# Four fused transformer blocks on one core: the first feed-forward's quantisation chain, its output bias, and the start of the second attention, reordered

## The chip, the cores and the metric

The kernel runs on one core of one Trainium2 chip. The metric is the device time of the program in microseconds (us); the kernel before takes 862.85 us (median of 3 runs, 858.54 to 864.74). One more execution was profiled; all traces here are of that one.

## The reference

Sixteen images of 16x16 tokens with 96 channels (4096 tokens) go through four blocks. Each block adds a mixing layer and a feed-forward to the residual, both on a layer norm of it. The mixing layers are: attention in windows of 16 tokens (3 heads of 32), attention in 8x8 windows, and two Fourier mixers, the second with weights routed per image; the feed-forwards of blocks 2 to 4 are mixtures of 4 experts (2 used). The change concerns mostly block 1's feed-forward, two "bit linear" layers with quantised activations:

```python
def _quantize_activations_groupwise(x):      # 5 groups of rows; the 16th image stays zero
    for g in range(5):
        gamma = max(|x[g]|)                  # one number for a whole group of 3 images
        x[g] = clip(x[g] * 128 / (gamma + 1e-5), -128 + 1e-5, 128 - 1e-5)
h   = quantise(x @ sign(W1 - mean).T + b1)   # 96 -> 384
out = quantise(gelu(h) @ sign(W2 - mean).T + b2)   # 384 -> 96
```

Each group's maximum must be known over all of its tokens before any of its values can be used, twice. In block 4 the mixer's weights come from a small network on each image's mean: `routing = softmax((scale * relu(mean @ fc1)**2 + bias) @ fc2)`.

## The kernel before

The residual X stays in SBUF for the whole program (128 tokens by 96 channels in each of 32 tiles). Five instruction streams are written out by hand, one for each of TensorE (PE), VectorE (DVE), ScalarE (ACT), GpSimd (POOL) and the DMA queue of SyncE (SP). Each runs strictly in its written order, and semaphores alone order the streams against each other. So the order in which a stream is written decides what waits behind what.

Attention, mixers and expert layers run over 8 groups of 4 tiles (512 tokens), as a software pipeline: in the pass for group g, TensorE works on g-1, g and g+1, and statistics and layer norms are made for g+2 and g+3. A layer norm (`normalise`, L472 to L496) is a chain of eleven POOL instructions that waits for DVE's statistics (`bn_stats`, L895 for 4 tiles, L912 for 6); TensorE then transposes its result (L1401 for 4 tiles, L1424 for 6).

The first feed-forward runs over 5 groups q = 0 to 4 of 6 tiles (FG, FT), in a loop written in each stream. For group q:
- `ffn_stats(q)` on DVE, `normalise` on POOL, `ffn_turn(q)` on PE, `ffn_hi` on ACT (L608) and `ffn_lo` on DVE (L917) split the normalised input in two parts.
- `ffn_up(q, j)`, j = 0 to 5 (L1434, L1435): first product; `ffn_y1` on ACT (L675) moves it out of PSUM and adds b1.
- First scale: `first_max` on DVE three times (L924), a small reduce (L1119), a PE transpose of the 128 row maxima (L1623), the maximum of that row on DVE (L1123), a PE product with ones that spreads it to all partitions (L1626), three small DVE instructions (L1132 to L1136), then three clips (L1140).
- gelu on ACT, three times (L697), then `down(q, t)`, t = 0 to 5: the bias b2 by a product with ones (L1565) and the second product (L1568). `ffn_out` on ACT (L681) copies it to the one buffer Y2.
- Second scale: the same chain again, one step later in the loop: L1084, L1578, L1088, L1582, L1092 to L1095, clip L1097, and L1099 adds the result to X.

In pass q of the loop DVE does `ffn_lo(q + 1)` first, the first scale of group q, and, in between, the second scale of group q - 2. TensorE does `ffn_up(q + 1)`, `down(q - 1)` and the products of both chains. After the loop come the last second scales, and then `attention(2, 1)`: it begins on DVE with the statistics of its group 2 and the softmax of group 0 (maximum L947, subtraction L953, exponential on ACT L625, sum L959, division L965).

Mixer 3 (block 4, `mixer3` in each stream) has, per group, a routing chain: `route_in` on PE (L1838), `routing_relu` on ACT (L815, L817), `routing_star` on DVE (L1293), `route_logits` on PE (L1847). On ACT `routing_relu` stands behind `mix_image(g, p, 0)` (L780), which waits for the first half of `mix_dft` on PE (L1754); on DVE `routing_star` is the last of the pass, behind `mix_x` (L1256) and `routing_out` (L1317); on PE `route_logits` is the last of the pass, right behind `mix_dft`.

Of the kernel before, what the change touches and what calls it, by code (L numbers as in the profile page):

```python
# [24 lines left out]
GT = 4  # L25
# [26 lines left out]
def program(nc, a, out):  # L52
    ctx = ExitStack()
    with ctx:
# [68 lines left out]
        gmx = sb("gmx", [1, 2])  # L123
# [4 lines left out]
        Y2 = sb("Y2", [P, FT, C])  # L128
# [70 lines left out]

        FT_BANKS = (slice(0, 2), slice(5, 7))  # L200

        def turned(m):
# [11 lines left out]
        CW = Y2[0:NF].rearrange("p t c -> p (t c)")[:, 0:8 * HF]  # L214
# [30 lines left out]
        ft_pe, fh_a, fl_v, fu_pe, y1_a, ab_v, gm1_v, gm2_v, g1_pe, g2_pe = (  # L245
            sem(n) for n in ("ft_pe", "fh_a", "fl_v", "fu_pe", "y1_a", "ab_v", "gm1_v", "gm2_v", "g1_pe", "g2_pe"))
        qs1_v, qs2_v, zero_p, y2_a = (sem(n) for n in ("qs1_v", "qs2_v", "zero_p", "y2_a"))
# [52 lines left out]
        def after(eng, s, value):  # L300

            if not (isinstance(value, int) and value <= 0):
                eng.wait_ge(s, value)

# [47 lines left out]
        def _(sp):  # L352
            with nc.allow_non_contiguous_dma(reason="small weights"):
# [11 lines left out]
                sp.wait_ge(zero_p, 1)  # L365
                sp.dma_start(b2bc[0:1, :], a["L0_ffn_b2"].rearrange("(a n) -> a n", a=1)).then_inc(wffn, 16)
# [100 lines left out]
        def _(pool):  # L467
            pool.memset(b2bc[:], 0.0).then_inc(zero_p, 1)
# [115 lines left out]
        def _(act):  # L584
# [93 lines left out]
            def ffn_out(q):  # L678
                act.wait_ge(fd_pe, 2 * q + 2)
                after(act, xu[1], q)  # L680
                act.activation(Y2[:].rearrange("p (u t) c -> p u (t c)", u=2), PS[:, 3:5, 0:3 * C], ACT.Copy).then_inc(y2_a, 1)  # L681
# [3 lines left out]
            for q in range(FG):  # L685
# [14 lines left out]
            act.activation(qT[0:C, :], bank(0, 512, C), ACT.Copy, scale=QSCALE).then_inc(q_a, 1)  # L700
# [141 lines left out]
            def mixer3(g, p):  # L842
# [24 lines left out]
        def _(dve):  # L867
# [58 lines left out]
            def attention(phase, ka, prev):  # L926
# [12 lines left out]
                def body(g, p):  # L939
                    n, m = 8 * ka + g, 8 * ka + g  # L940
                    if has(g, 3, 2, PREPS[phase]):
# [3 lines left out]
                    if has(g, 1):  # L945
# [11 lines left out]
                    if has(g, 1):  # L957
# [15 lines left out]
                    if ka == 0 and isinstance(g, int):  # L973
# [108 lines left out]
            def second_max(r):  # L1082
                dve.wait_ge(y2_a, r + 1)
                dve.tensor_reduce(am1[:, 1:2], Y2[:], AX.XY, ALU.max, apply_absolute_value=True).then_inc(gm2_v, 1)  # L1084

            def second_row(r):
                dve.wait_ge(g2_pe, 2 * r + 1)
                dve.tensor_reduce(gmx[:, 1:2], PS[0:1, 7, 256:256 + P], AX.X, ALU.max).then_inc(gm2_v, 1)  # L1088

            def second_scale(r):  # L1090
                dve.wait_ge(g2_pe, 2 * r + 2)
                dve.tensor_scalar(qe[:, 1:2], PS[:, 7, 384:385], QEPS, 1.0 / QB, ALU.add, ALU.mult).then_inc(qs2_v, 1)  # L1092
                dve.wait_ge(qs2_v, 2 * r + 1)
                dve.reciprocal(qs[:, 1:2], qe[:, 1:2])
                dve.tensor_scalar(ql[:, 1, :], qc[:], qe[:, 1:2], None, ALU.mult).then_inc(qs2_v, 1)  # L1095
                dve.wait_ge(qs2_v, 2 * r + 2)
# [901 lines left out]
```

## Time and profile before

| | us |
|---|---|
| median of 3 runs | 862.85 |
| profiled execution | 860.89 |
| its span, first to last instruction | 859.1 |
| busy in the span: PE, DVE, POOL, ACT | 779.6, 589.5, 556.4, 428.5 |
| first feed-forward, first clip to the first transpose of attention 2 that follows it | 98.03 to 167.37 |
| mixer 3, first to last `route_logits` of its loop | 631.4 to 693.7 |

The rows further down come from views of one trace. A timeline row gives the start and the length of a run of like instructions, and in brackets how long the engine stood idle before it and what released it. A row of groups gives count, busy time, mean nanoseconds, and the idle time before. A row of stretches gives, for each engine, busy time and count, and the TensorE clock granted (PEclk: 1.00 is 2.4 GHz, 0.50 is 1.2 GHz).

### The profile page before, as it was taken

How to read it: one execution, taken by the hardware profiler on the slowest of the kernel's cores; microseconds unless marked ns; L12 is line 12 of the kernel's file. 1: busy time of each engine (PE TensorE's matmuls, PEld its weight loads, DVE VectorE, ACT ScalarE, POOL GpSimd, SP SyncE). 2: the span in 40 equal slices, each digit the busy share in tenths (PEclk: the TensorE clock that was granted, in tenths of full speed). 3: DMA queues.
4: the chain of work that ended last, by engine and by line, in shares of the span. 5: the costliest groups of instructions: out<-in, count | busy, mean ns of one | idle time of the engine just before them, and what ended most of it. 6: DMA issues, size and time to landing. Idle time of an engine off the chain costs nothing.

```text
span 859.1 us, 27761 instructions
## 1 busy us (share of the span) xinstructions
PE 779.6 (91%) x10760; PEld 641.8 (75%) x10760; DVE 589.5 (69%) x1609; ACT 428.5 (50%) x777; POOL 556.4 (65%) x885
## 2 busy tenths in 40 slices
PE   4897678699899999969997999999799999999996
PEld 3776566588688888958876688888777776888886
DVE  6677477678577777848874477787776773776754
ACT  3564563366544444457773553535445555444441
POOL 5645523455287887867773687788565674788764
PEclk9696698799999999989998999999967999999999
DMA  6611100000311101000011011010000011110030
GB/s 165 125 12 30 35 1 2 2 3 3 78 54 36 50 28 29 3 1 2 0 46 30 28 31 30 27 56 3 2 1 2 0 29 29 33 55 27 28 84 20
DMA packets 39145, 26.17 MB, mean 30 GB/s; under 512 B 27132, under 2 KB 31981, under 8 KB 39045
## 3 DMA queue, kind: packets, MB, share of 16 engines
q1 hardware_dynamic: 38302, 24.41, 11.2%
q8 instruction: 68, 1.11, 0.6%
q10 hardware_dynamic: 742, 0.38, 0.2%
q14 instruction: 33, 0.26, 0.1%
HBM read 7.87 MB, written 1.57 MB: 11 GB/s over the span
## 4 chain that ended last, share of the span: by engine, by line
PE 81%; DVE 10%; ACT 3%; issue 3%; POOL 2%; POOLq 0%; ACTq 0%; DVEq 0%
PE PS L1679 22%; PE PS L1652 9%; PE PS L1653 8%; PE PS L1656 4%; PE PS L1401 3%; PE PS L1767 3%; PE PS L1754 3%; PE PS L1387 3%; PE PS L1778 2%; PE PS L1787 2%; PE PS L1388 2%; PE PS L1797 2%; PE PS L1568 2%; PE PS L1480 2%; PE PS L1847 1%
## 5 line engine op out<-in xcount | busy, mean ns | idle before, releaser
L712 ACT ACTIVATE H<-PS,B 128x512 f32<-128x512 f32 x288 | 173.7, 690 | 194.7 <-PE PS L1656 194.7
L1679 PEld LDWEIGHTS PS<-M,H 128*64 128x64 f32 x4608 | 192.3, 137 | 21.7 <-issue 17.5
L1679 PE MATMUL PS<-M,H 128*64 128x96 f32 x4608 | 205.1, 248 | 1.8 <-DVE X L1196 1.8
L1196 DVE SCALAR_TENSOR_TENSOR X<-PS,G,X 128x96 f32<-128x96 f32 (+1 forms) x384 | 121.7, 318 | 96.6 <-PE PS L1679 86.3
L480 POOL TENSOR_TENSOR msum<-stats 128x4 f32<-128x4 f32 (+1 forms) x61 | 16.1, 263 | 137.7 <-DVE stats L895 111.3
L1652 PE MATMUL PS<-XH,M1h 128*128 128x512 f32 x192 | 78.7, 410 | 0.0
L490 POOL TENSOR_TENSOR XN<-X,mean 128x384 f32<-128x384 f32 x56 | 47.0, 840 | 48.9 <-PE PS L1401 48.9
L1653 PE MATMUL PS<-FHL,M1l 128*128 128x512 f32 x192 | 77.3, 402 | 0.0
L516 POOL TENSOR_TENSOR PF<-G,B 128x1536 f32<-128x1536 f32 x24 | 66.2, 2759 | 10.2 <-DVE G L1187 10.2
L524 POOL TENSOR_TENSOR ex<-euler,dl 128x16 f32<-128x16 f32 x24 | 69.9, 2912 | 1.7 <-DVE dl L1160 1.6
L494 POOL TENSOR_TENSOR rs<-ve,half 128x4 f32<-128x4 f32 (+1 forms) x61 | 65.4, 1072 | 4.8
L1401 PE MATMUL PS<-ident,XN 128*96 128x128 f32 x224 | 39.8, 307 | 17.3 <-POOL XN L496 17.3
L895 DVE BATCH_NORM_STATS2 stats<-X 128x6 f32<-128x96 f32 (+1 forms) x224 | 41.1, 244 | 15.0 <-POOL XN L496 12.6
L496 POOL TENSOR_TENSOR XN<-XN,rs 128x384 f32<-128x384 f32 x56 | 47.4, 847 | 4.4
L604 ACT ACTIVATE XH<-PS 96x512 fp32r<-96x512 f32 x56 | 33.1, 591 | 33.4 <-PE PS L1401 33.0
L900 DVE TENSOR_TENSOR XL<-PS,XH 96x512 fp32r<-96x512 f32 x56 | 38.1, 680 | 16.7 <-ACT XH L604 16.7
L551 POOL TENSOR_TENSOR H<-H 96x128 f32<-96x128 f32 x64 | 29.6, 492 | 28.3 <-DVE H L1345 28.3
L1652 PEld LDWEIGHTS PS<-XH,M1h 128*128 128x128 f32 x192 | 36.7, 191 | 13.4 <-ACT H L712 5.4
L1652 PE MATMUL PS<-FHL,M1h 128*128 128x512 f32 x96 | 43.5, 453 | 3.2 <-ACT H L712 3.2
L530 POOL TENSOR_TENSOR X<-X,PF 128x384 f32<-128x384 f32 (+1 forms) x24 | 24.3, 1012 | 32.5 <-DVE X L1196 32.5
L519 POOL TENSOR_TENSOR PF<-PF 128x768 f32<-128x768 f32 x24 | 43.7, 1823 | 1.9
L1156 DVE TENSOR_TENSOR gs<-gs 128x16 f32<-128x16 f32 x24 | 42.8, 1782 | 0.8
(245 smaller groups left out, 1818.3 us busy)
## 6 DMA issues: line engine op xcount, KB each, us to landing
FHL<-XH SPq DMA_DIRECT2D x36, 192.0 KB, 2.5
FHL<-XL SPq DMA_DIRECT2D x36, 64.0 KB, 2.1
X<-XH SPq DMA_DIRECT2D x12, 192.0 KB, 2.5
raw<-L_ffn_w SPq DMA_DIRECT2D x3, 576.0 KB, 5.1
M<-L_ffn_w SPq DMA_DIRECT2D x3, 576.0 KB, 5.0
XH<-XL SPq DMA_DIRECT2D x24, 64.0 KB, 1.9
out<-X SPq DMA_DIRECT2D x8, 192.0 KB, 2.6
X<-x SPq DMA_DIRECT2D x3, 384.0 KB, 6.7
```

The source lines that it names most:

```text
L490: pool.tensor_tensor(xn, x, rows(mean), ALU.subtract).then_inc(part, 1)
L494: pool.tensor_tensor(rs[:, 0:n], ve[:, 0:n], half[:, 0:n], ALU.pow).then_inc(part, 1)
L496: pool.tensor_tensor(xn, xn, rows(rs), ALU.mult).then_inc(done, 1)
L516: pool.tensor_tensor(GB, G[:].unsqueeze(3).to_broadcast([P, GT, EXP, C]), B2[e][:].unsqueeze(1).to_broadcast([P, GT, EXP, C]), ALU.mult).t ...
L519: pool.tensor_tensor(GB[:, :, 0:2, :], GB[:, :, 0:2, :], GB[:, :, 2:4, :], ALU.add).then_inc(gb_p, 1)
L524: pool.tensor_tensor(ex[:, :, :].rearrange("p t e -> p (t e)"), euler[:], dl[:, :, :].rearrange("p t e -> p (t e)"), ALU.pow).then_inc(gex ...
L712: act.activation(H[p][:, c, :], bank(UB[c]), ACT.Gelu, bias=B1[e][:, c:c + 1]).then_inc(gelu_a, 1)
L1196: ins = dve.scalar_tensor_tensor(xt(g, t), bank(4 + t % 2)[:, e * C:(e + 1) * C], G[:, t, e:e + 1], xt(g, t), ALU.mult, ALU.add)
L1401: ins = pe.transpose(o, XN[:, t, :], ident[:])
L1652: pe.matmul(bank(UB[c]), M1h[e][:, cs], XS[p][j], start=True, stop=False)
L1653: pe.matmul(bank(UB[c]), M1l[e][:, cs], XS[p][k], start=False, stop=False)
L1679: ins = pe.matmul(Y[rows, x * C:(x + 1) * C], H[p][:, j, t * P + rows.start:t * P + rows.stop], M2[e][:, j, :], start=c == 0, stop=c == CH ...
```

## The change

In the feed-forward, the second scale of group q - 2 joins the first scale of group q: one transpose of two columns, one row maximum over two partitions, one small diagonal product, one spreading product. The order of DVE and PE within a pass is new. The bias b2 leaves TensorE and is added by POOL (for the last group by DVE), b2 is loaded to all partitions by one broadcast DMA, and Y2 gets a second buffer. `ffn_out` stands behind the gelus. `ffn_stats(2)` moves into the last steps of attention 1. The first scores and the first softmax of attention 2 move between the last two chains of the feed-forward, ahead of the statistics of its group 2. In mixer 3, `routing_relu` moves ahead of both `mix_image` calls on ACT, and `mix_x` moves behind `routing_out` and `routing_star` on DVE.

```diff
 # SP
-                sp.wait_ge(zero_p, 1)
-                sp.dma_start(b2bc[0:1, :], a["L0_ffn_b2"].rearrange("(a n) -> a n", a=1)).then_inc(wffn, 16)
+                sp.dma_start(b2bc[:], a["L0_ffn_b2"].partition_broadcast(P)).then_inc(wffn, 16)
 # POOL
-            pool.memset(b2bc[:], 0.0).then_inc(zero_p, 1)
...
-            for q in range(FG):
+            def ffn_rows(q):
                 normalise(q, EPS_T, FT, fst_v, fag_p, X[:, q * FT * C:(q + 1) * FT * C], FX, ft_pe, fxn_p)
+            def ffn_bias(r):
+                pool.wait_ge(y2_a, r + 1)
+                pool.tensor_tensor(Y2[r % 2], Y2[r % 2], b2bc[:].unsqueeze(1).to_broadcast([P, FT, C]), ALU.add).then_inc(y2_p, 1)
+            for q in range(4):
+                ffn_rows(q)
+            ffn_bias(0)
+            ffn_rows(4)
+            ffn_bias(1)
             prep(2, 1, 0)
+            ffn_bias(2)
+            ffn_bias(3)
             prep(2, 1, 1)
 # ACT
             def ffn_out(q):
                 act.wait_ge(fd_pe, 2 * q + 2)
-                after(act, xu[1], q)
+                after(act, xu[1], q - 1)
...
                 if q == FG - 1:
                     prep_hi(8, 0)
-                if q > 0:
                     ffn_out(q - 1)
                 for c in range(CH):
                     ... gelu ...
+                if 0 < q < FG - 1:
+                    ffn_out(q - 1)
...
-            ffn_out(FG - 1)
             prep_hi(9, 1)
             attention(2, 1)
 # ACT, mixer3
-                if has(g, 1):
-                    mix_image(g, p, 0)
                 if has(g, 2, 2):
                     routing_relu(g + 2)
                 if has(g, 1):
+                    mix_image(g, p, 0)
                     mix_image(g, p, 1)
 # DVE, attention 1, g == GROUPS - 1 (the add to X of the last group is in the step behind it)
                             for c in range(CH):
                                 first_max(0, c)
+                            ffn_stats(2)
 # DVE, feed-forward (the old loop leaves; see L1102 to L1147)
+            def scale_rows(q):
+                n = columns(q).stop - columns(q).start     # 1 or 2 chains
+                dve.wait_ge(g_pe, 2 * q + 1)
+                dve.tensor_reduce(gmx[0:n], PS[0:n, 7, 0:P], AX.X, ALU.max).then_inc(gm_v, 1)
+                if n == 2:
+                    dve.wait_ge(gm_v, chain(q) + 3)
+                    dve.tensor_scalar(gdg[:], ident[0:2, 0:2], gmx[:], None, ALU.mult).then_inc(gm_v, 1)
+            for q in range(FG):
+                if q > 0:
+                    for c in range(CH):
+                        first_max(q, c)
+                if q >= 2:
+                    second_max(q - 2)
+                dve.wait_ge(ab_v, 3 * (q + 1))
+                dve.tensor_reduce(am1[:, 0:1], am[:, 0, 0:CH], AX.X, ALU.max).then_inc(gm_v, 1)
+                if q == 0:
+                    dve.wait_ge(fu_pe, 6)
+                    ffn_lo(1)
+                if q + 3 < FG:
+                    ffn_stats(q + 3)
+                if q >= FG - 2:
+                    dve.wait_ge(fxn_p, FG)
+                    prep_stats(8 + q - (FG - 2), q - (FG - 2), (xu[1], q - (FG - 2) + 1), None)
+                scale_rows(q)
+                if 0 < q and q + 2 < FG:
+                    dve.wait_ge(fu_pe, 6 * (q + 2))
+                    ffn_lo(q + 2)
+                if q == FG - 1:
+                    prep_lo(8, 0)
+                scales(q)
+                clip_first(q)
+                if q >= 2:
+                    add_second(q - 2)
+                if q == 0:
+                    dve.wait_ge(fu_pe, 12)
+                    ffn_lo(2)
+            second_max(FG - 2)
+            dve.wait_ge(s_pe, 9)
+            dve.tensor_reduce(top, scores(1), AX.X, ALU.max).then_inc(mx_v, 1)
+            scale_rows(FG)
+            dve.wait_ge(mx_v, 9)
+            dve.tensor_tensor(scu, scores(1), top..., ALU.subtract).then_inc(sub_v, 1)
+            scales(FG)
+            add_second(FG - 2)
             prep_lo(9, 1)
+            for u in range(2):
+                dve.wait_ge(fd_pe, 2 * FG - 1 + u)
+                ... Y2[0] half u = PSUM + b2bc ...
+            second_max(FG - 1)
+            dve.wait_ge(exp_a, 9)
+            dve.tensor_reduce(sm[:], scv, AX.X, ALU.add).then_inc(sum_v, 1)
+            scale_rows(FG + 1)
+            ... reciprocal rc, PFC = scv * rc ...
+            scales(FG + 1)
+            add_second(FG - 1)
+            prep_stats(10, 2, (xu[1], 2), None)
             attention(2, 1, (xu[1], FG))
 # DVE, mixer3
-                if has(g, -1):
-                    mix_x(1, g - 1, xu[6])
                 if has(g, 1, 2):
                     routing_out(g + 1, 1 - p)
                 if has(g, 2, 2):
                     routing_star(g + 2)
+                if has(g, -1):
+                    mix_x(1, g - 1, xu[6])
 # PE, down: the product of ones and b2bc leaves; feed-forward loop
             ffn_turn(1)
             for q in range(FG + 1):
+                more = q + 1 < FG
+                if q == 0:
+                    maxima(0)
                 if q == FG:
                     first_products()
+                if more:
+                    for j in range(3):
+                        ffn_up(q + 1, j)
+                if q > 0:
+                    down(q - 1, 0)
+                if q + 2 < FG:
+                    ffn_turn(q + 2)
+                if q == FG - 1:
+                    pe.wait_ge(fl_v, FG)
+                    prep_turn(8, True)
+                if more:
+                    ffn_up(q + 1, 3)
+                if 0 < q < FG:
+                    down(q - 1, 1)
+                if more:
+                    ffn_up(q + 1, 4)
+                    ffn_up(q + 1, 5)
+                if q > 0:
+                    maxima(q)
+                if q == FG:
+                    pe.wait_ge(y2_a, FG - 1)
+                    pe.wait_ge(q_a, 9)
+                    pe.wait_ge(k_a, 9)
+                    head_scores()
+                    down(q - 1, 1)
+                if q > 0:
+                    down(q - 1, 2)
+                spread(q)
+                if q > 0:
+                    for t in range(3, FT):
                         down(q - 1, t)
             prep_turn(9, True)
+            maxima(FG + 1)
+            spread(FG + 1)
             attention(2, 1)
```

`maxima(q)` waits for DVE's reduces and transposes one or two columns of row maxima; `spread(q)` waits for `scale_rows(q)` and multiplies by ones; `scales(q)` waits for it and makes the scales; `clip_first` holds the three clips, `add_second` the second clip and the add to X.

## Rows read from the trace of the kernel before

**Rows 1.** The chain of waits, 84 to 172 us: shares by line.
```profile
by line: PE PS L1568 15.6%; PE PS L1434 10.9%; issue 8.7%; PE PS L1565 8.5%; PE PS L1435 7.2%; DVE H L1140 5.2%; PE PS L1424 4.8%; DVE FHL L917 4.1%; ACT H L697 4.1%; PE PS L1387 3.2%; PE PS L1480 2.7%; DVE Y L1097 2.0%; PE PS L1582 1.9%; D
```

**Rows 2.** Stretches between clip starts: length; busy PE, PEld, DVE, ACT, POOL; PEclk, DMA.
```profile
98.03:111.79 13.76, 10.98 (x115) 9.00 (x117) 7.14 (x19) 7.13 (x11) 6.49 (x15) 0.75 0.00 1
111.79:123.61 11.82, 9.30 (x125) 7.34 (x122) 8.88 (x20) 7.20 (x11) 5.38 (x7) 1.00 0.00 1
123.61:136.94 13.33, 10.32 (x121) 7.93 (x116) 9.41 (x23) 6.54 (x10) 0.34 (x3) 0.87 0.01 1
136.94:148.60 11.66, 8.31 (x114) 6.87 (x109) 9.15 (x23) 4.09 (x6) 5.56 (x15) 0.85 0.01 1
148.60:167.37 18.77, 12.19 (x178) 9.49 (x177) 12.38 (x27) 7.71 (x11) 8.51 (x18) 0.83 0.01 1
```

**Rows 3.** Timeline, all engines, at the start of the feed-forward.
```profile
86.02 0.55 DVE L956 TENSOR_TENSOR X<-X,PS 128x384 f32<-128x384 f32 x1
87.13 1.06 DVE L912 BATCH_NORM_STATS2 stats<-X 128x6 f32<-128x96 f32 x6 [0.56 <-POOL H L496]
...
87.20 1.49 PE L1424 MATMUL PS<-ident,H 128*96 128x128 f32 x6 [1.23 <-DVE X L956]
```

**Rows 4.** Groups by line and engine, 84 to 172 us.
```profile
L675 ACT ACTIVATE H<-PS,b1c 128x384 f32<-128x384 f32 x26 | 14.8, 581 | 12.8 <-PE PS L1435 12.0
L924 DVE TENSOR_REDUCE am<-H 128x1 f32<-128x768 f32 x14 | 13.0, 939 | 0.6 <-ACT H L675 0.6
...
L1140 DVE TENSOR_SCALAR H<-H,ql 128x768 f32<-128x768 f32 x15 | 9.3, 675 | 0.2
...
L1099 DVE SCALAR_TENSOR_TENSOR X<-Y,qs,X 128x576 f32<-128x576 f32 x5 | 4.1, 818 | 0.2
L917 DVE TENSOR_TENSOR FHL<-PS,FHL 96x768 fp32r<-96x768 f32 x4 | 3.8, 949 | 1.4 <-ACT FHL L608 1.4
...
L1084 DVE TENSOR_REDUCE am<-Y 128x1 f32<-128x576 f32 x5 | 3.7, 744 | 0.9 <-ACT Y L681 0.9
...
L681 ACT ACTIVATE Y<-PS 128x576 f32<-128x576 f32 x5 | 3.3, 651 | 13.3 <-PE PS L1568 13.3
L608 ACT ACTIVATE FHL<-PS 96x768 fp32r<-96x768 f32 x4 | 3.2, 808 | 4.9 <-PE PS L1424 4.8
```

**Rows 5.** Timeline, from attention 2's statistics of group 2 to their transpose.
```profile
162.01 0.72 DVE L895 BATCH_NORM_STATS2 stats<-X 128x6 f32<-128x96 f32 x4
...
166.74 1.35 DVE L965 TENSOR_TENSOR PF<-SC,rc 128x768 f32<-128x768 f32 x1
...
167.37 1.06 PE L1401 MATMUL PS<-ident,XN 128*96 128x128 f32 x4
```

**Rows 6.** Timeline, a norm on POOL, a first gelu, and POOL beside clips.
```profile
88.27 0.20 POOL L480 TENSOR_TENSOR msum<-stats 128x6 f32<-128x6 f32 x1 [1.17 <-DVE stats L912]
...
92.71 1.15 POOL L496 TENSOR_TENSOR H<-H,rs 128x576 f32<-128x576 f32 x1
...
98.74 2.59 ACT L697 ACTIVATE H<-H,qs 128x768 f32<-128x768 f32 x3 [0.47 <-DVE H L1140]
...
113.08 1.58 POOL L490 TENSOR_TENSOR H<-X,mean 128x576 f32<-128x576 f32 x1
```

**Rows 7.** Waits in mixer 3, 636 to 712 us: total, times, longest.
```profile
PE PS L1847 <- DVE hh L1293: 3.5, 5, 0.8
```

**Rows 8.** Timeline of one group of mixer 3.
```profile
642.27 0.95 ACT L828 ACTIVATE RT<-PS 4x384 fp32r<-4x384 f32 x2
...
642.90 1.99 PE L1754 MATMUL PS<-sg,H 128*96 128x128 f32 x16
...
643.87 0.55 DVE L1317 TENSOR_TENSOR RT<-PS,RT 4x384 fp32r<-4x384 f32 x1
```

**Rows 9.** Stretches of mixer 3 between starts of `route_logits`, columns as in rows 2.
```profile
657.97:671.75 13.78, 13.18 (x98) 11.24 (x98) 7.96 (x26) 6.94 (x16) 7.87 (x20) 0.75 0.00 1
671.75:682.93 11.18, 10.23 (x99) 8.60 (x99) 9.12 (x26) 6.78 (x16) 6.76 (x17) 1.00 0.00 0
```

More of the change, by code:

```diff
@@ L303, in after, with chain @@
                 eng.wait_ge(s, value)
+        def chain(q):
+            return sum(2 + 2 * (2 <= x < FG) for x in range(q))
         def scores(ka):
@@ L940, in body @@
                     n, m = 8 * ka + g, 8 * ka + g
-                    if has(g, 3, 2, PREPS[phase]):
+                    head = ka == 1 and g < 0
+                    if has(g, 3, 2, PREPS[phase]) and not head:
                         prep_stats(m + 3, g + 3, prev, upd)
@@ L944, in body @@
                         prep_lo(m + 2, p)
-                    if has(g, 1):
+                    if has(g, 1) and not head:
                         dve.wait_ge(s_pe, n + 2)
@@ L956, in body @@
                         dve.tensor_tensor(xg(g - 1), xg(g - 1), bank(6, GT * C), ALU.add).then_inc(upd, 1)
-                    if has(g, 1):
+                    if has(g, 1) and not head:
                         dve.wait_ge(exp_a, n + 2)
@@ new lines, in scales @@
+            def scales(q):
+                s = columns(q)
+                n = s.stop - s.start
+                dve.wait_ge(g_pe, 2 * q + 2)
+                dve.tensor_scalar(qe[:, s], PS[:, 7, P:P + n], QEPS, 1.0 / QB, ALU.add, ALU.mult).then_inc(qs_v, 1)
+                dve.wait_ge(qs_v, 2 * q + 1)
+                if q < FG:
+                    after(dve, ge_a, 3 * q)
+                dve.reciprocal(qs[:, s], qe[:, s])
+                dve.tensor_tensor(ql[:, s, :], qc[:].unsqueeze(1).to_broadcast([P, n, 2]), qe[:, s].unsqueeze(2).to_broadcast([P, n, 2]),
+                                  ALU.mult).then_inc(qs_v, 1)
+                dve.wait_ge(qs_v, 2 * q + 2)
@@ L1140, in _, with add_second @@
                     dve.tensor_scalar(y, y, ql[:, 0, 0:1], ql[:, 0, 1:2], ALU.min, ALU.max).then_inc(cl_v, 1)
-            for r in range(FG - 2, FG):
-                second_max(r)
-                second_row(r)
-                second_scale(r)
-            prep_lo(9, 1)
+            def add_second(r):
+                dve.tensor_scalar(Y2[r % 2], Y2[r % 2], ql[:, 1, 0:1], ql[:, 1, 1:2], ALU.min, ALU.max).then_inc(y2_v, 1)
+                dve.wait_ge(y2_v, r + 1)
+                dve.scalar_tensor_tensor(x6(r), Y2[r % 2], qs[:, 1:2], x6(r), ALU.mult, ALU.add).then_inc(xu[1], 1)
@@ L1435, in ffn_up, with head_scores @@
                 pe.matmul(bank(j % 3, 3 * P), w, FL[0:C, us], start=False, stop=True).then_inc(fu_pe, 1)
+            def head_scores():
+                for t in range(GT):
+                    for w, rows in enumerate(HALF):
+                        ts = slice(t * P + w * 64, t * P + (w + 1) * 64)
+                        for h in range(HEADS):
+                            hs = slice(h * DH, (h + 1) * DH)
+                            ins = pe.matmul(scores(1)[rows, t, h], qT[hs, ts], KT[hs, ts], start=True, stop=True)
+                ins.then_inc(s_pe, 1)
             def attention(phase, ka):
@@ L1451, in body @@
                         ffn_turn(0)
-                    if more:
+                    if more and not (ka == 1 and isinstance(g, int) and g == -1):
                         pe.wait_ge(q_a, n + 2)
@@ L1460, in body @@
                                 pe.wait_ge(bias_a, 1)
[L1461 to L1464 removed]
+                        if ka == 0:
+                            for t in range(GT):
+                                for w in range(P // bs):
+                                    rows, ts = slice(w * bs, (w + 1) * bs), slice(t * P + w * bs, t * P + (w + 1) * bs)
                                     ins = pe.matmul(scores(0)[rows, t // 2, t % 2], qT[:, ts], kT[:, :, ts], start=True, stop=True)
[L1466 to L1470 removed]
+                            ins.then_inc(s_pe, 1)
+                        else:
+                            head_scores()
                     if has(g, 0):
@@ L1541, in body @@
                     if has(g, 3, 2, PREPS[phase]):
-                        prep_turn(m + 3, ka == 1 and has(g, 3))
+                        prep_turn(m + 3, ka == 1 and has(g, 3), (qs_v, 2 * (FG + 1) + 1) if ka == 1 and g == -1 else None)
                     if ka == 0 and isinstance(g, int) and g == GROUPS - 1:
```

157 lines of the change are left out of this document (47 added, 110 removed).

## The prediction, made before the changed kernel had run

> **What bounds the kernel now.** I read the chain of waits first. Over the program it is mostly TensorE, but the change touches two places only. Cut to the 88 us around the first feed-forward the chain is mixed: products, the bias products (L1565, 8.5%, so 7.5 us), DVE's clips and gelu take turns, with 8.7% of "issue" between them [rows 1]. That is the latency of a loop, not a busy engine. So I cut the stage at the starts of the first clips, C0 to C4 (98.03, 111.79, 123.61, 136.94, 148.60), and at the first transpose of attention 2 after it (167.37). The passes take 13.76, 11.82, 13.33 and 11.66, and the tail 18.77 [rows 2]; no engine fills them. DVE, which carries both scale chains, is busy 7.1 to 9.4 us of each pass. The question per pass is what ends last once the two chains are one.
>
> **The change, part by part.** Times below are relative to the clip start of the pass.
>
> *Start.* `ffn_stats(2)` now stands on DVE ahead of the last add to X of attention 1, and waits for POOL's norm. Today the add runs at 86.02, the statistics at 87.13 to 88.19 and TensorE's transposes start at 87.20 [rows 3]. New: statistics, add (0.55), transposes at about 88.8, 1.6 later. The later `ffn_stats(3)` no longer stands between spread and scale, which gives back part; I take C0 + 0.8, bounds 0 and +1.6.
>
> *Pass 0 to 1.* No second chain runs here yet, before or after. The bias products leave: 7.5 us over five passes, 1.5 each [rows 1]. 13.76 - 1.5 = 12.3; bounds 10.5 and 13.8.
>
> *Passes 2 to 3 and 3 to 4.* With `ffn_lo` done ahead of the clip, TensorE's first products run while gelu runs, and DVE's own order becomes the limit: three clips 1.86, second clip and add with the hand-over 1.45 (the add 0.82), three maxima at 0.9 (2.7), second maximum 0.75, small reduce 0.16, statistics of attention 2 0.72, row maximum 0.28, diagonal 0.2, the wait for the spread 0.4, scale instructions 0.52: 9.0 [rows 4, 5]. (The diagonal is new; nearest row any of the tiny DVE instructions, 0.14 to 0.21.) In pass 3 to 4 a 0.68 `prep_lo` partly fills the wait: 9.4. Savings 13.33 - 9.0 = 4.3 and 11.66 - 9.4 = 2.3.
>
> *Pass 1 to 2.* Here I see a new wait. POOL's queue now reads rows 0 to 3, bias(0), rows 4. bias(0) waits for `ffn_out(0)`, which ACT does behind the gelus of group 1. Gelu starts 0.71 after the clip and lasts 2.59 [rows 6], `ffn_out` 0.65 [rows 4], bias(0) at least 1.15 (a POOL instruction of the same size [rows 6]): POOL is free at 5.2. The norm of group 4, whose statistics lie ready since the pass before, runs only then: 5.6 from its first to its last instruction (88.27 to 93.86 [rows 6]), so to 10.8. TensorE waits in `ffn_turn(4)` from about 3.9, with the rest of the first products, the maxima and the spread queued behind. From 10.8: turn 0.8, products 3 to 5 and one `down` 2.1 (both as the chain has them at full clock), `ffn_y1` 0.6, `ffn_hi` 0.8, `ffn_lo` 0.95 [rows 4], scales 0.55 end at 16.6; TensorE's 2.9 of it doubles at half clock, 19.5. After 7 idle us it will start at half, and full clock may return on the way, so I take 17.8, short of the middle: against 11.82 a loss of 6.0, bounds 4.8 and 7.7. Today this norm runs beside the clips of group 1 (L490 at 113.08 [rows 6]) and nobody waits for it.
>
> POOL's bias also meets DVE: the same instruction took 1.58 beside the clips instead of 1.15 [rows 6], so bias(3), issued beside the clips of group 4, gets 1.5. The Trainium skill (SBUF — State Buffer, "SBUF: two separate sides") says the pair of ports that GpSimd and VectorE share is held by one of them for its whole instruction. By that rule alone, had each of four biases to sit out one 0.82 us instruction, the sum would be 3.3 worse; the row shows 0.43 for one.
>
> *Tail.* Today attention 2's statistics of group 2 run on DVE at 162.01 [rows 5], 13.41 after C4, and POOL's norm and the transpose follow at 167.37 while DVE does the first softmax beside them. New, DVE must do that softmax first: clips 1.86, add 1.45, second maximum 0.75, maximum of scores, subtraction and sum at 0.95 each, row maxima 2 x 0.28, scales 2 x 0.5, add 1.45, `prep_lo` 0.68, the last bias from PSUM 0.8, second maximum 0.75, division 0.23 + 1.35, add 1.45, is 15.2 without one wait [rows 4, 5]; with the wait for the scores (gelu of group 4 is held by `ffn_out(3)`, so the scores end near 5.8) and hand-overs it is 17.5. Then 5.36 from statistics to transpose as today [rows 5], now with nothing beside it: 22.9 against 18.77, a loss of 4.1; bounds 1.8 and 8.4 (the latter with TensorE at half clock up to the scores). The softmax was no wait of TensorE before, so moving it forward buys nothing behind the transpose.
>
> Sum of the feed-forward: +0.8 - 1.5 + 6.0 - 4.3 - 2.3 + 4.1 = +2.8.
>
> *Mixer 3.* TensorE waits for `routing_star` before `route_logits` in five groups, 3.5 us in all [rows 7]. In one of them: `routing_hi` on ACT ends at 643.22, `mix_dft` runs 642.90 to 644.89, `routing_out` takes 0.55 [rows 8]. New order: relu and square need only `route_in`, so they end near 643.7, `routing_out` starts 0.6 earlier, where `mix_x` stood, and the star is done near 644.5, before `mix_dft` ends. The gap closes: -3.5, bounds 0 and -4. `mix_x` and `mix_image` lose nothing that TensorE waits for.
>
> *At nothing:* the broadcast of b2 and the dropped POOL memset lie in the start-up, ahead of the transposes of W1 and W2, which wait for the same semaphore behind TensorE's first products; without that cover they would cost what a broadcast takes to land, a few us once.
>
> Sum: 860.89 + 2.8 - 3.5 = 860.2 for the profiled execution. That one lies 2.0 below the median of 862.85, so 862.2 for the median, in effect no change.
>
> **Rivals.** (1) *Faster by the clock in mixer 3.* Groups at full clock take 11.18, one at a mean of 0.75 takes 13.78 [rows 9]; of the five groups three lie below full clock, by some 5 us together. If the gaps at `route_logits` cause the falls, closing them gives up to 5 more: 857. For: each fall comes some microseconds behind such a gap. Against: two of the five gaps are followed by none.
>
> (2) *Slower by the clock in the last passes.* Without bias products TensorE has six `down` and a turn, some 4 us of work, in the 9.4 of pass 3 to 4. If it is then at half clock, the three `down` before `ffn_out(3)`, the first products and the scores of attention 2 take twice as long, the maximum of scores starts near 10.3 instead of 5.9, and the tail gives 4.4 more; with half clock in passes 1 and 2 too, another 2. That gives 867 to 869. It decides from the point where TensorE's wait for gelu in pass 3 to 4 drops the clock. For: mean clocks of 0.75 to 0.87 in passes with such waits; against: 1.00 in pass 1 to 2, which has one of 2.5 us [rows 2]. The Trainium skill (TensorE: Matmul & The Clock Gate, "HAM oscillation") holds that idle stretches between bursts return the array to half clock; by that rule this rival holds.
>
> (3) *No stall at `ffn_turn(4)`:* the loss of 6.0 falls away, because `ffn_out(0)` comes early enough: 856. For: it would need only gelu's 2.6 us of ACT ahead of it to be over sooner; against: the order leaves no way round bias(0).
>
> (4) *Mixer 3 does not do what it says:* the star is held by another instruction, so that gain is 0: 866. Against: both its producers are early [rows 8].
>
> **Numbers.** Forecast 0.54, rival 1 0.17, rival 2 0.15, rival 3 0.06, rival 4 0.08. The forecast alone spans 858 to 867. The range goes down to 853, where rivals 1 and 3 add, and up to 870, the end of rival 2 with its bounds. One per cent, some 8.6 us, is about what a measurement of this kernel tells from no change. Faster by more needs rival 1 in full and the small ends of the losses: 0.16. Slower by more needs rival 2 with the upper bounds elsewhere: 0.13. Within: 0.71.
>
> **What would show it.** In the profile after: TensorE idle for some 7 us before the transposes of group 4, with POOL's bias then norm ahead of them; clip starts about 9 us apart in the two last passes and over 16 us in the one before; attention 2's statistics of group 2 some 17 us behind the last clips with POOL's norm alone after them; no wait at `route_logits`. I am wrong if the third pass is not the longest, if the tail is not longer than 18.77, or if mixer 3 gains other than about 3.5 at equal clocks.

## The result, and the profile after

The changed kernel takes 857.64 us (median of 20 runs), the kernel before 863.78 us on the same chips: a ratio of 0.9931, 95% interval 0.9903 to 0.9958. It is 6 us, or 0.7%, faster. That lies in the predicted range (853 to 870) and within one per cent; it is still a gain that the measurement can tell from none, where the forecast was 0.7 us, in effect none. The profiled execution has a span of 855.9 us against 859.1.

Two rows of the page of the kernel after (busy time of each engine; shares of the chain that ended last), and then the second of them for the kernel before: TensorE's share of that chain falls from 81% to 73%, GpSimd's rises from 2% to 8%. Not all of that is the change: a second profile of the kernel before (before_again, below) has 78% and 5%.

```profile
PE 769.2 (90%) x10631; PEld 632.8 (74%) x10631; DVE 576.9 (67%) x1602; ACT 426.6 (50%) x776; POOL 560.1 (65%) x888
...
PE 73%; DVE 11%; POOL 8%; issue 4%; ACT 4%; POOLq 0%; ACTq 0%; DVEq 0%
```

```profile
PE 81%; DVE 10%; ACT 3%; issue 3%; POOL 2%; POOLq 0%; ACTq 0%; DVEq 0%
```

The stretches between the first clips of the groups, and from the last of them to attention 2's transpose of group 2, in the kernel after (columns as in [rows 2], which they answer):

```profile
97.80:110.26 12.46, 9.68 (x94) 8.07 (x95) 7.94 (x19) 7.89 (x12) 2.97 (x3) 0.73 0.01 1
110.26:128.79 18.53, 9.44 (x69) 7.45 (x70) 7.00 (x14) 6.96 (x11) 6.49 (x12) 0.65 0.00 0
128.79:137.32 8.53, 7.17 (x93) 5.79 (x93) 7.92 (x19) 6.16 (x10) 2.50 (x7) 0.97 0.01 2
137.32:146.93 9.61, 5.86 (x79) 4.60 (x77) 8.99 (x20) 3.75 (x5) 5.78 (x7) 0.80 0.01 2
146.93:170.51 23.58, 13.85 (x188) 10.81 (x185) 14.30 (x31) 8.37 (x12) 9.56 (x23) 0.79 0.00 1
```

The passes are those of the prediction: 12.46, 18.53, 8.53, 9.61 and 23.58 us, forecast at 12.3, 17.8, 9.0, 9.4 and 22.9. The long one is the stall that was foreseen. The timeline of all engines shows it in one reading: the bias of group 0 on GpSimd, behind it the norm of group 4 from first to last instruction, then TensorE's transposes after 6.22 idle us, and VectorE's row maximum after 9.89.

```profile
114.17 1.41 POOL L579 TENSOR_TENSOR Y<-Y,b2bc 128x576 f32<-128x576 f32 x1 [13.25 <-ACT Y L697]
115.54 0.20 POOL L484 TENSOR_TENSOR msum<-stats 128x6 f32<-128x6 f32 x1
...
119.97 1.15 POOL L500 TENSOR_TENSOR H<-H,rs 128x576 f32<-128x576 f32 x1
121.17 1.51 PE L1476 MATMUL PS<-ident,H 128*96 128x128 f32 x6 [6.22 <-POOL H L500]
126.31 0.28 DVE L1111 TENSOR_REDUCE gmx<-PS 2x1 f32<-2x128 f32 x1 [9.89 <-PE PS L1640]
```

The tail is as foreseen too; its rows answer [rows 5]. The statistics of group 2 come last on VectorE, and the norm on GpSimd has nothing beside it until TensorE starts.

```profile
165.18 0.73 DVE L910 BATCH_NORM_STATS2 stats<-X 128x6 f32<-128x96 f32 x4
...
169.63 0.82 POOL L500 TENSOR_TENSOR XN<-XN,rs 128x384 f32<-128x384 f32 x1
170.51 1.09 PE L1453 MATMUL PS<-ident,XN 128*96 128x128 f32 x4 [5.54 <-POOL XN L500]
```

So this kernel stands 3.1 us *behind* the one before at that transpose (170.51 against 167.37, [rows 5]). It then loses 5.3 more in the next two groups of attention 2, which the prediction did not have: 11.68 and 9.23 us at half and mixed clock, where the kernel before (the second pair of rows) took 8.53 and 7.04.

```profile
170.51:182.19 11.68, 11.09 (x166) 9.39 (x167) 6.04 (x14) 4.08 (x7) 5.37 (x18) 0.50 0.02 4
182.19:191.42 9.23, 9.23 (x184) 8.01 (x184) 5.73 (x11) 4.57 (x8) 2.85 (x4) 0.72 0.01 2
```

```profile
167.37:175.90 8.53, 7.94 (x168) 6.82 (x167) 6.52 (x15) 4.96 (x9) 4.09 (x11) 0.77 0.01 4
175.90:182.94 7.04, 7.04 (x185) 6.12 (x184) 5.38 (x10) 4.56 (x8) 4.09 (x11) 1.00 0.02 5
```

All of that and more comes back in mixer 3. Its groups, cut at the transposes in each, take 9.93 us at full clock without a microsecond of idle (busy 9.93 of 9.93), against 11.18 with waits at full clock and 13.78 at 0.75 before ([rows 9], cut at the logits):

```profile
644.41:654.34 9.93, 9.93 (x100) 8.57 (x98) 7.80 (x26) 6.80 (x16) 8.22 (x19) 1.00 0.01 2
...
664.27:674.19 9.92, 9.92 (x100) 8.57 (x98) 7.93 (x27) 6.79 (x16) 8.31 (x20) 1.00 0.00 0
```

One group on the timeline, answering [rows 8]: the star ends at 650.43 while TensorE's `mix_dft` still runs to 651.08, and the logits follow without a wait. The table of waits of this stretch, where [rows 7] had 3.5 us, is empty.

```profile
648.45 0.95 ACT L844 ACTIVATE RT<-PS 4x384 fp32r<-4x384 f32 x2
649.09 1.99 PE L1823 MATMUL PS<-sg,H 128*96 128x128 f32 x16
649.58 0.55 DVE L1369 TENSOR_TENSOR RT<-PS,RT 4x384 fp32r<-4x384 f32 x1
650.15 0.28 DVE L1345 TENSOR_SCALAR hh<-hq,msb 24x2 f32<-24x2 f32 x1
```

From the first transposes of mixer 3's pipeline to the first ones of the experts behind it, this trace takes 93.98 us (633.24 to 727.22) and the one before 106.67 (623.77 to 730.44). One trace of each thus reads as 8.5 lost by the feed-forward and some 12.7 gained in mixer 3. The experiments ask whether those are the prices of the two parts.

### The profile page after: what moved, and what is told of

The parts are those of the page before. It is cut to its first block, busy times and chain, and to the rows that moved or that the text cites. A ratio compares the mean times of both kernels' runs of the same rounds, so it can differ in the third digit from the quotient of the medians.

```text
span 855.9 us, 27491 instructions
## 1 busy us (share of the span) xinstructions
PE 769.2 (90%) x10631; PEld 632.8 (74%) x10631; DVE 576.9 (67%) x1602; ACT 426.6 (50%) x776; POOL 560.1 (65%) x888
## 3 DMA queue, kind: packets, MB, share of 16 engines
q1 hardware_dynamic: 38444, 24.46, 11.2%
## 4 chain that ended last, share of the span: by engine, by line
PE 73%; DVE 11%; POOL 8%; issue 4%; ACT 4%; POOLq 0%; ACTq 0%; DVEq 0%
PE PS L1748 22%; PE PS L1721 8%; PE PS L1722 7%; PE PS L1725 3%; PE PS L1453 3%; PE PS L1823 3%; PE PS L1439 2%; PE PS L1836 2%; PE PS L1856 2%; PE PS L1847 2%; PE PS L1866 2%; PE PS L1440 2%; PE PS L1539 2%; POOL H L555 2%; POOL rs L498 1%
## 5 line engine op out<-in xcount | busy, mean ns | idle before, releaser
L484 POOL TENSOR_TENSOR msum<-stats 128x4 f32<-128x4 f32 (+1 forms) x61 | 16.1, 265 | 101.1 <-DVE stats L910 84.0
L1453 PE MATMUL PS<-ident,XN 128*96 128x128 f32 x224 | 38.3, 297 | 23.0 <-POOL XN L500 22.9
L910 DVE BATCH_NORM_STATS2 stats<-X 128x6 f32<-128x96 f32 (+1 forms) x224 | 41.0, 245 | 19.4 <-POOL XN L500 17.2
L1453 PEld LDWEIGHTS PS<-ident,XN 128*96 128x96 f32 x224 | 24.9, 134 | 28.9 <-POOL XN L500 14.2
```

The source lines that it names most:

```text
L1453: ins = pe.transpose(o, XN[:, t, :], ident[:])
```

## The experiments

Ratios are to the kernel before, timed beside each kernel on the same chip, with 95% intervals.

**Each part alone.** *m3_only* is the kernel before with these two moves; *ffn_only* is the kernel after with them undone.

```diff
 # ACT
+routing_relu(g + 2)
 mix_image(g, p, 0)
-routing_relu(g + 2)
 mix_image(g, p, 1)
 # DVE
-mix_x(1, g - 1, xu[6])
 routing_out(g + 1, 1 - p)
 routing_star(g + 2)
+mix_x(1, g - 1, xu[6])
```

> The kernel before with the routing order of mixer 3 alone (relu and square ahead of both images on ScalarE, the update of X last on VectorE). Theory 1 (two large terms cancel in the change): the order is worth far more than the 3.5 us of waits, because with no wait left TensorE keeps the full clock; the groups of mixer 3 then take 9.9 us each as in the kernel after, against a mean of 12.2 before, in all 12 to 14 us: ratio 0.984 to 0.986, some 850 to 852 us. Rival (as predicted): the waits alone, 3.5 us, ratio 0.996, 860 us, with some groups still below full clock.

> The kernel after with mixer 3 in the order of before, so the feed-forward part of the change alone. Theory 1: the first feed-forward costs 3 us up to the transposes of attention 2's group 2, and the half clock behind them, through attention 2's next two groups, another 5: 8.5 us in all, ratio 1.010, 872 us; mixer 3 again with groups of 11 to 14 us. Rival (as predicted): 2.8 us, ratio 1.003, 866.5 us, and the slow groups of attention 2 in the one profile of after were chance.

Measured: mixer 3 alone 0.9941 (0.9905 to 0.9977), about -5 us; the feed-forward alone 0.9979 (0.9948 to 1.001), about -2 us. Together they give the whole change. Neither theory 1 nor the rival holds for the feed-forward: both said slower, and its interval ends at +0.9 us. For mixer 3 the value lies between the two; the interval (-8 to -2 us) excludes the -12 of theory 1 and holds the -3.5 of the rival. In the stretches of m3_only the mechanism is all there (one group still below full clock, then 9.93 each). The profiled execution took 848.91 us, where the median of this kernel is 857.35, so it shows more than the median gains:

```profile
634.88:645.48 10.60, 10.60 (x100) 9.04 (x99) 8.04 (x26) 6.57 (x15) 8.00 (x19) 0.94 0.01 2
645.48:655.41 9.93, 9.93 (x100) 8.57 (x98) 7.80 (x26) 6.80 (x16) 8.23 (x19) 1.00 0.01 3
```

**Which half of the routing order.** *relu_only* has the lines of ACT, *star_only* those of DVE.

> The kernel before with ScalarE's half of the routing order alone (relu and square ahead of both images); on VectorE the update of X stays ahead of the router's output and of the star. Theory: the star waited for ScalarE's square, 0.7 us, so this half does nearly all: the wait ahead of the logits falls from 0.7 to 0.2 us or none, mixer 3 takes 95 to 99 us, ratio 0.993 to 0.995. Rival: VectorE's order holds the star as long, the wait stays at 0.5 or more, ratio 0.998 to 1.000.

> The kernel before with VectorE's half of the routing order alone (the update of X last). Theory: the star waits for ScalarE's square, which still stands behind the first image, so the wait ahead of the logits stays at 0.5 us or more in each group: no gain, ratio 0.999 to 1.001, mixer 3 at 102 to 107 us. Rival: VectorE's half had a share in the wait, it falls to 0.3 or less, ratio 0.995.

Measured: relu_only 0.995 (0.9909 to 0.9991), star_only 0.9988 (0.9946 to 1.0029). TensorE's waits in mixer 3, first of relu_only (its lines stand one lower), then of star_only:

```profile
PE PS L1846 <- DVE hh L1292: 1.0, 2, 0.7
```

```profile
PE PS L1847 <- DVE hh L1293: 3.3, 5, 0.7
```

ScalarE's half removes the wait in three groups of five and brings most of the time; VectorE's half alone removes next to nothing, since the star waits for ScalarE's square, and closes the last two only beside the other. By the waits both theories hold, but for the one of 0.7 that stays in relu_only; by the medians alone their rivals (0.998 and 0.995) lie inside the intervals.

**The same programs again.** *before_again* and *after_again* are the two kernels unchanged, in a second profile.

> The kernel before, unchanged, in a second profile. Theory (its first profile had a favourable clock in the first feed-forward): of the kernels with this feed-forward three were profiled so far besides it, and the four passes took 50.6, 50.7, 55.1 and 63.5 us; a second profile of the same program gives passes that differ by 2 us or more from 13.76, 11.82, 13.33 and 11.66, with other mean clocks, while stretches at full clock repeat within 0.1 us. Rival: the passes repeat within 0.5 us, and the differences came from the edits of mixer 3.

> The kernel after, unchanged, in a second profile. Theory: the pass from the second to the third clip stays at 18 us or more (the wait for the norm is in the order of GpSimd's queue) and the tail at 22 or more; attention 2's groups 2 and 3, 20.9 us in the first profile, and mixer 3, 94.0, vary by several us with the clock. Rival: they repeat within 0.5 us.

Before_again shows what the base of the feed-forward's sum is worth. The stretches of the kernel before, second profile (columns and cuts as in [rows 2]):

```profile
96.59:111.65 15.06, 12.29 (x115) 9.90 (x117) 7.15 (x18) 7.22 (x11) 6.49 (x15) 0.66 0.01 1
111.65:124.98 13.33, 10.81 (x126) 8.57 (x122) 8.88 (x20) 7.42 (x11) 5.38 (x7) 0.87 0.01 1
124.98:139.82 14.84, 11.82 (x121) 8.99 (x116) 9.42 (x24) 6.44 (x10) 0.34 (x3) 0.77 0.00 1
139.82:153.60 13.78, 10.56 (x113) 8.88 (x108) 9.62 (x23) 3.77 (x6) 6.83 (x19) 0.63 0.01 1
153.60:172.38 18.78, 12.38 (x179) 9.58 (x178) 12.39 (x27) 8.02 (x11) 6.75 (x14) 0.83 0.01 1
```

The same program, the same instructions, DVE and ACT busy within 0.5 us of the first profile, and the four passes take 57.0 us instead of 50.6, at mean clocks of 0.63 to 0.87 instead of 0.75 to 1.00. All stretches that were profiled, in us, worked out as above (attention 2: its two groups behind the transpose):

| kernel | first to last clip | tail | attention 2 | mixer 3 |
|---|---|---|---|---|
| before | 50.6 | 18.8 | 15.6 | 106.7 |
| before_again | 57.0 | 18.8 | 15.6 | 105.8 |
| star_only (feed-forward of before) | 50.7 | 18.8 | 15.7 | 108.2 |
| m3_only (feed-forward of before) | 50.7 | 18.8 | 15.6 | 97.4 |
| relu_only (feed-forward of before) | 55.1 | 18.8 | 15.5 | 98.6 |
| m3_fill (feed-forward of before) | 63.5 | 18.8 | 14.3 | 103.4 |
| after | 49.1 | 23.6 | 20.9 | 94.0 |
| after_again | 48.7 | 22.1 | 16.0 | 97.1 |
| ffn_only | 48.8 | 22.1 | 16.0 | 102.5 |
| rows_first | 44.1 | 23.6 | 16.4 | 97.0 |
| stats_early | 51.4 | 18.7 | 14.6 | 97.1 |
| fill | 51.4 | 23.6 | 14.0 | 96.7 |
| both | 41.6 | 17.1 | 15.5 | 98.6 |
| both_fill | 40.0 | 17.2 | 16.1 | 97.1 |

Clips plus tail average 73.4 us over the six traces with the old feed-forward (69.3 to 82.2) and 71.5 over the three with the new one (70.8 to 72.7). These averages do not settle the sign: without the 82.2 of m3_fill the old ones are at 71.6, and with attention 2's two groups added the old and the new stand at 88.7 and 89.1. What the part is worth is read from the median of ffn_only. What the traces show is the spread. The old loop runs at a clock that changes from execution to execution: its passes take 50.6 or 50.7 in three traces and 55.1, 57.0 and 63.5 in the others, so the trace that the prediction used lies at the low end, while the new loop's take 48.7 to 51.4 in the five traces that leave its order as it is. The rival of before_again falls. After_again bears its theory out: the pass of the stall is 18.54, the tail 22.12, attention 2's groups are back at 16.0. The 20.9 of the first trace was one outcome of the clock; after_again took 851.28 us, where the median of the kernel after is 857.64, so its 16.0 need not be the usual one.

**The stall in the queue of GpSimd.**

```diff
-            ffn_bias(0)
             ffn_rows(4)
+            ffn_bias(0)
```

> The kernel after with GpSimd's norm of row group 4 ahead of the bias of group 0 in its queue. Theory: TensorE's 6.2 us of idling ahead of the transposes of group 4 goes, and the half clock behind it; the pass from the second to the third clip falls from 18.5 to about 9.5 us, and the kernel by 8 to 9 us against after: ratio to before 0.983, 849 us. Rival: the bias of group 0, now behind the norm, becomes late itself and VectorE waits for it in the second maximum: the pass stays at 14 or more, 4 us at most are won, ratio 0.989. Rival 2: what is won is lost to the clock in the next passes: 0.

Measured: 0.9813 (0.9754 to 0.9873), 847.97 us. The pass is 12.76 us instead of 18.53, at a clock of 0.62; TensorE goes from `down` to the transposes of group 4 without idling, and bias(0) comes no later than `ffn_out(0)` lets it. The wait is the one that the theory named, and both rivals fall. The pass was to take 9.5, though: it stays longer, at a mean clock that does not rise without the idling (0.62, against 0.65 in after), and the same pass of both_fill (below) takes 10.23 even at 1.00. Of the 10 us between the two medians this pass shows 5.8; the intervals of the two ratios leave some 5 to 16 open.

```profile
114.08:126.84 12.76, 9.88 (x69) 7.87 (x70) 6.99 (x14) 6.96 (x11) 1.40 (x1) 0.62 0.00 0
```

**The tail.**

```diff
             add_second(FG - 2)
+            prep_stats(10, 2, (xu[1], 2), None)
             prep_lo(9, 1)
...
             add_second(FG - 1)
-            prep_stats(10, 2, (xu[1], 2), None)
```

> The kernel after with attention 2's statistics of group 2 moved ahead of the low half of group 1 on VectorE, so that GpSimd's norm runs beside the last scale chain. Theory: the transposes of group 2 start at about 165 instead of 170.5, 5.5 us earlier, and without that idling TensorE is back at full clock some groups of attention 2 earlier, another 3 to 5 us: 8 to 10 us in all, ratio to before 0.982 to 0.984. Rival 1 (only the latency): 5.5 us, ratio 0.987, the groups of attention 2 behind it at half clock as in after. Rival 2: another wait (the division, the last add to X) holds the transposes or what follows them, 2 us or less.

Measured: 0.9858 (0.9817 to 0.9899), 853.09 us. The tail is 18.65 instead of 23.58 or 22.1, and attention 2's two groups take 14.6 instead of 20.9 or 16.0: the theory's direction, with 3.5 to 5 us from the wait and 1 to 6 from the clock, by which of the two traces of after it is held against. The transposes came at 171.5, not at 165, since the passes ahead of them took longer in this trace. The interval holds the theory's 0.984 and rival 1's 0.987 alike, so the median does not say what the clock adds.

**TensorE's clock by itself.** *fill* adds only work that nobody reads:

```diff
+  pe.wait_ge(qs_v, 2 * (FG + 1) + 1)
+  for _ in range(28):
+      pe.transpose(PS[:, 7, 2 * P:3 * P], ident[:], ident[:])
   prep_turn(m + 3, ...)          # attention 2, group 2
```

> The kernel after with 28 transposes of the identity on TensorE, written to free columns and read by nobody, ahead of the transposes of attention 2's group 2: TensorE works where it idled for 5.5 us, and nothing that anybody waits for comes earlier. Theory (the clock): the full clock is back sooner, attention 2's groups 2 and 3 take 15 to 16 us instead of 20.9, the transposes start as before or up to 1 us later: 3 to 5 us less than after, ratio to before 0.987 to 0.990. Rival (the latency alone counts, the slow groups were chance): as after or 1 us more, 0.993.

Measured: 0.9925 (0.9889 to 0.9961), as the change without it (0.9931). The tail is 23.58 as in the trace of after, so nothing comes earlier; the two groups behind it are the shortest of all 14 traces:

```profile
172.76:179.67 6.91, 6.32 (x166) 5.45 (x167) 5.33 (x11) 4.08 (x7) 4.08 (x11) 1.00 0.02 6
179.67:186.72 7.05, 7.05 (x184) 6.13 (x184) 5.93 (x14) 4.54 (x8) 4.09 (x11) 1.00 0.01 3
```

TensorE idled there 0.89 us instead of 5.54, and the same work ran at 1.00 instead of 0.50 and 0.72. The gap did not bring the clock down, though. In the trace of after TensorE is at half clock from 163.5 on, and the gap lasts from 164.97 to 170.51; full clock returns at 187.4:

```profile
149.90:163.40 13.50, 9.31 (x151) 7.55 (x150) 8.96 (x19) 6.47 (x9) 5.48 (x12) 1.00 0.01 2
163.60:170.51 6.91, 1.37 (x4) 0.45 (x3) 2.24 (x8) 1.56 (x3) 4.09 (x11) 0.50 0.00 0
170.51:187.30 16.79, 16.20 (x270) 13.89 (x272) 8.55 (x17) 5.76 (x11) 8.22 (x22) 0.50 0.01 3
187.50:191.42 3.92, 3.92 (x81) 3.31 (x77) 3.23 (x8) 2.69 (x5) 0.00 (x0) 1.00 0.02 4
```

In the trace of fill the clock is at half from 162.7 on, and full clock returns at 169.5, while the filling runs (167.83 to 171.87):

```profile
162.80:169.40 6.60, 5.12 (x17) 3.89 (x18) 5.22 (x14) 2.19 (x4) 1.02 (x6) 0.50 0.00 0
169.60:172.76 3.16, 2.27 (x21) 2.03 (x20) 0.00 (x0) 0.00 (x0) 2.95 (x5) 1.00 0.00 0
```

So with the gap filled the full clock came back sooner, in one trace. The gap is not the whole of it: both_fill (below) does not have it and runs its first group behind these transposes at 0.70. That the clock is worth 3 us in the median is not shown; the median is the rival's 0.993.

*m3_fill* puts work into the gap of mixer 3 of the kernel before, with its old order:

```diff
+  for _ in range(5):
+      pe.matmul(PS[96:128, 7, 2 * P:3 * P], ident[:, 96:128], ident[:], start=True, stop=True)
   route_logits(g + 2)
```

> The kernel before with 5 matmuls of the identity on TensorE (32 rows that nobody reads) ahead of the router's logits in each group of mixer 3, where TensorE idled 0.6 to 0.8 us; the wait for VectorE stays. Theory (the gaps bring the clock down): the groups of mixer 3 stay at full clock and take 10.8 to 11.2 us each, the mixer 98 to 101 us instead of 102 to 107: 4 to 6 us less, ratio 0.993 to 0.995. Rival (the falls come from elsewhere): the mixer stays at 102 to 107 us, ratio 1.000.

Measured: 1.0026 (0.999 to 1.0062). The filling was too long (a group's takes 1.28 us, the gap it fills 0.7), so each group pays 0.5 us or so for it, and the groups of 11.2 to 12.5 us still hold one at 0.88. Mixer 3 takes 103.4 us, at a mean clock of 0.95 against 0.87; the median does not confirm a gain (both numbers are the rival's), and this run's first feed-forward was the slowest of all. What share of mixer 3's gain is the clock's thus stays open.

**A better version.** *both* has the moves of rows_first and stats_early; *both_fill* adds idle transposes in the feed-forward, and from the third step of the loop on a wait for `ffn_lo` ahead of the products:

```diff
+  if 1 < q < FG: pe.wait_ge(fl_v, min(q + 2, FG))
+  if q == 1: idle_work(3, 16)                    # 16 transposes into a free bank
   for j in range(3): ffn_up(q + 1, j)            # if a group is left
+  if 1 < q < FG: idle_work(5, (0, 0, 11, 4, 11)[q])
   down(q - 1, 0)
```

> The kernel after with both moves: the norm of row group 4 ahead of the bias of group 0 on GpSimd, and attention 2's statistics of group 2 ahead of the low half of group 1 on VectorE. Theory: the two gains add, since they lie in different stretches (pass from the second to the third clip 12.8 instead of 18.5 us, tail 18.7 instead of 23.6, and attention 2's first two groups 15 instead of 16 to 21): 10 and 5 us against after, ratio to before 0.975, 842 us. Rival: the clock that comes back in one stretch is lost in the other, only the waits add: ratio 0.980.

> The kernel with both moves, and transposes of the identity on TensorE that nobody reads (16 in the first pass, 11, 4 and 11 in the next ones) where it idles 3.8, 2.9, 1.1 and 2.9 us in the first feed-forward. Theory (the clock in the passes follows TensorE's idling, and half clock there is paid for on the loop): the first two passes, 12.5 and 11.5 us at mean clocks of 0.73 and 0.74, come to 11 and 10 at full clock; 3 us less than with both moves alone, ratio to before 0.973. Rival 1 (the loop's latency lies on VectorE and ScalarE, the clock is off it): no change, 0.977. Rival 2: the fillings last too long where the clock is at half and delay the products: 2 us more, 0.979.

Measured: both 0.9768 (0.9716 to 0.9819), 843.75 us; both_fill 0.9719 (0.9683 to 0.9755), 838.14 us, by its ratio 24 us below the kernel before. In the trace of both the two waits are gone together (passes 41.6, tail 17.1); its interval holds the theory's 0.975 and the rival's 0.980 alike, so whether the gains add in full stays open. The first two passes, of both and then of both_fill:

```profile
98.15:110.69 12.54, 9.77 (x94) 8.12 (x95) 7.94 (x19) 7.96 (x12) 8.12 (x14) 0.73 0.01 1
110.69:122.14 11.45, 8.55 (x69) 6.76 (x70) 7.00 (x15) 6.97 (x11) 1.41 (x1) 0.74 0.01 1
```

```profile
98.26:110.43 12.17, 10.20 (x105) 8.27 (x103) 8.04 (x20) 8.05 (x12) 8.10 (x14) 0.86 0.01 1
110.43:120.66 10.23, 8.45 (x105) 7.12 (x104) 7.00 (x15) 6.85 (x11) 1.41 (x1) 1.00 0.01 2
```

The clock rises to 0.86 and 1.00, and the passes fall by 0.4 and 1.2 us: a gain from the clock, 1.6 of the 3 that were expected there, in one trace of each. The rest of the 4 us between the two spans (840.1 and 836.1) lies in later stages, and the intervals of the two ratios overlap.

## Why the prediction was right, and where not

The time was right for reasons that are half the predicted ones, and partly by luck. The forecast was no change; the gain of 6 us lies inside the range because the range is 17 us wide. The 857 of rival 1 meets the measured 857.64 by chance: it was made of +2.8 for the feed-forward and -8.5 for mixer 3, and the parts alone measure -2 and -5. (Rivals 1 and 3 together give 851 by the prediction's own terms, not the 853 that it put down as the lower end.)

**The loop's structure: right.** Every pass of the trace came within 0.75 us of its term: the passes at +0.2, +0.7, -0.5 and +0.2, the tail at +0.7, with the stall where and why it was foreseen. Rows_first and stats_early confirm both causes by taking them away.

**The base of the feed-forward's sum: wrong.** Its +2.8 was made against the one trace at hand. Passes and tail of after's trace sum to 72.7, 3.4 above the 69.3 of [rows 2]; the terms behind the start had said +2.0. But 69.3 lies at the low end: the second profile of the same kernel took 75.8, in an execution of 865.02 us, near the 864.47 that is this kernel's median beside it, where the first profile was of one of 860.89. The part alone measures -2 us (-4.5 to +0.9), not +2.8. That the base is the whole of the difference is argued from these traces; no run holds the clock fixed. What the step lacked is a price for the clock in the loop of *before*; the prediction had the means of 0.75 to 0.87 in [rows 2] and used them for its rival 2 only.

**Start, +0.8: not decided.** The first clip came at 97.80 against 98.03, but in the 14 traces it lies between 95.2 and 104.5, at mean clocks of 0.78 to 0.86 up to it.

**Mixer 3, -3.5: mechanism right, size too small.** The wait went from 3.5 to 0, by ScalarE's half as [rows 8] had it. The part alone is worth -5 us (-8 to -2). In the table, the four traces without ScalarE's half and with nothing added average 105.8 us and the eight with the whole new order 96.9, a difference of 8.9, which lies beyond the interval's end and which so few traces, some of them far from their kernel's median, cannot sharpen. At equal full clock a group went from 10.5 to 11.2 down to 9.93, so five groups give 3 to 6 us. The rest goes with falls of the clock that became rarer. That the gaps cause these falls, rival 1's mechanism, is not shown: with the gaps filled m3_fill still has a group at 0.88. Nor is it a rule that without the wait none comes: rows_first has mixer groups of 11.53 us at 0.85 and 11.04 at 0.89 with no such wait.

**Rival 2 (half clock in the last passes): its mechanism came, in three traces of five.** Of the five with this order of the tail, after, rows_first and fill ran their last pass at 0.69 to 0.80, the maximum of scores came 7.7 us behind the last clip, and the tail took 23.6; after_again and ffn_only had 1.00 there, 6.2 and 22.1. That is 1.5 us, not 4.4.

**Attention 2 behind the tail: missed.** The prediction priced the tail as latency alone. The groups behind it took between 0.4 us (16.0 against 15.6) and 5.3 more than in the kernel before, by how long the half clock lasted in them. That the longer idling of the new tail causes this is not shown: the clock fell ahead of the gap (see fill), and the kernel before also idles 4.18 us just there, ahead of attention 2's first products, and has 0.77 in its first group:

```profile
164.73 0.71 PE L1387 MATMUL PS<-XH,WAh 96*96 96x512 f32 x1 [4.18 <-DVE SC L953]
```

**The bias on GpSimd** cost 1.41 us each, above the 1.15 taken as its least and near the 1.5 taken beside clips; it decided nothing but the stall. In the trace of after bias(3) came at 150.29, behind the clips of group 4 and not beside them, and the 1.58 that the prediction took for the same instruction is that of another one of its size (L490 in [rows 6]). Where clips and a norm on GpSimd did meet, VectorE's three clips took 2.37 us instead of 1.86 and GpSimd's subtraction 1.26 instead of 0.82:

```profile
137.32 2.37 DVE L1132 TENSOR_SCALAR H<-H,ql 128x768 f32<-128x768 f32 x3
138.01 1.26 POOL L494 TENSOR_TENSOR XN<-X,mean 128x384 f32<-128x384 f32 x1
...
153.15 0.82 POOL L494 TENSOR_TENSOR XN<-X,mean 128x384 f32<-128x384 f32 x1
```

The Trainium skill (SBUF — State Buffer, "SBUF: two separate sides") has one of the two engines hold the shared pair of ports for its whole instruction. The rows agree that both engines pay; they show about 0.5 us for each in this meeting.

## What to carry to other kernels

Where one engine runs a latency loop with gaps, its clock, and so the loop's time, can differ by more than 10% between executions of one program; make the sum against several traces, or weigh each stretch with its granted clock, before calling a change of 3 us a loss. In a queue that runs in order, put work whose inputs lie ready ahead of work that waits for a late one: one exchanged pair of lines was worth 10 us here, more than the whole change. Two waits of TensorE that were removed here brought more than their length by the medians, 3.5 us of them in mixer 3 some 5 and 6.2 us ahead of group 4 some 10, but both intervals (2 to 8, 5 to 16) hold the bare wait too.

## What the runs showed of the hardware

The half clock can last long after TensorE has gone back to work. In the trace of after TensorE works from 170.51 on with one pause of 0.59 us, and yet runs at 0.50 up to 182.19 and at a mean of 0.72 over the group after; after 28 idle transposes in the same gap the same work runs at 1.00 from its first group on.

Executions of one program differ. The two profiles of the kernel before have spans of 859.1 and 863.2 us and differ in the clock of the loop, while stages at full clock repeat: five successive groups of the first expert layer took 17.13 to 17.15 us each in both profiles. The Trainium skill (TensorE: Matmul & The Clock Gate, "Part 1: The HAM clock gate") says that the number of slow products at a kernel's start differs from run to run; the two profiles of the kernel before show it far inside the kernel, with 6.4 us of difference over four passes.
